# Scratch layout, load shapes and store order around two attention stages of one kernel

## The chip, the cores and the metric

The kernel runs on one core of one Trainium2 chip. Its time is the device time of one execution in microseconds (us). Three runs of the kernel before took 1209.68, 1210.88 and 1212.73 us; the median is 1210.88 us. Engines are named as the profile names them: PE (TensorE matmul), PEld (weight load), DVE (VectorE), ACT (ScalarE), POOL (GpSimd) and SP (SyncE). A small q behind a name (SPq, ACTq) is the engine's sequencer, which issues DMAs.

## The reference

An input x of 2 batches x 1024 tokens x 128 channels passes through four residual layers, all in float32:

```
x = x + attention_a(layernorm(x))      # 16 heads of 8 channels, causal, latent k and v,
                                       # and a 32-channel rotary q.k term shared by all heads
x = x + experts(layernorm(x))          # 8 experts, each takes its top 257 tokens of a batch
x = x + attention_b(layernorm(x))      # 16 heads of 8 channels, causal, plain q, k, v;
                                       # k is reinterpreted by a reshape before q.k
x = x + experts(layernorm(x))
```

In attention_a, `scores = (q.k + q_rope.k_rope) / sqrt(8 + 32)`; q, k and v are products of the normalised x (or of its latent projection) with 128 x 128 weights, reshaped to 16 heads of 8. In attention_b k goes through a transpose and a reshape to (1024, 8), so that a key row of a head is made of other tokens' channels.

## The kernel before

Each attention is one block with two stages, whose kind is "a" or "b". In `project_stage` DVE and ACT normalise x, PE turns it in four chunks of 512 tokens and multiplies it by the weights, ACT copies q and k out of PSUM, rounded to a narrow format, and DVE stores what the rounding left over. So `q_hl` and `k_hl` hold two parts each (0 and 1) as [128 channels, part, 2048 tokens]; for kind "a" the rotary parts `r_hl` lie in the first 64 rows of the third q buffer.

The attention works on 8 groups (2 batches x 4 groups of 4 heads). For each it wants a q tile and a k tile of [128 rows, 4 heads, 1024 tokens] in which the contraction runs down the rows: rows 0 to 95 are three slots of the 32 rotary rows, rows 96 to 119 are three slots of the 8 channels of a head, with parts (0, 0, 1) for q and (0, 1, 0) for k; row 120 holds the row maximum (for q) or ones. The channel rows of a head have to change their partition, and this is done through DRAM: SP stores q_hl, k_hl and r_hl to `scratch_q`, `scratch_k` (kind "b": `scratch_kb`) and `scratch_r` (`store`, L464 to L478), and `load_group` (L293 to L306) brings one group back into one of three buffers: one DMA per slot and side, 12 DMAs for a group of kind "a" whose rotary rows are loaded too, 6 without them. All these DMAs are issued by SP, in its program order: first the stores of group 0 alone, a wait for them, the loads of group 0, then the stores of the three other groups of batch 0, the stores of batch 1, a wait for batch 0, the loads of group 1, and inside `attention_stage` (L538) the maxima of half 1 (`m_rows`), a wait for batch 1 and the loads of group 2.

In `attention_stage` PE first computes the scores of a half (a group and 512 queries) to find their maxima (`max_piece`, L625, reduced on DVE, L762), turns the maxima, DVE copies them, and a DMA (`m_rows`, L535, from ACT for the first half) puts them in row 120. Then it computes the scores again, transposed (`score_unit`, L668), ACT takes the exponential (L739), POOL zeroes the masked triangle, and PE multiplies by v (`values`, L686). A table fixes which max pieces of later halves stand beside which score unit; three score banks let PE run three units ahead of ACT. For kind "a" the rotary rows are loaded for one head, and ACT (group 0, q, L727) or POOL (L581 for group 0, L554 for the next ones) copies them to the other three heads before PE may use the tile. The exponentials are written into the memory of q_hl and k_hl (tiles `pt`), so ACT waits before its first one for all stores of both batches (L728 ff.).

## Time and profile before

| what | value |
|---|---|
| median of three runs | 1210.88 us |
| profiled execution | 1209.04 us, of which the span on the core is 1207.3 us |
| PE busy | 1039.5 us, 86% of the span |
| DVE, ACT, POOL busy | 594.8, 572.0 and 241.9 us |
| DMA | 39.95 MB in 29916 packets, 33 GB/s over the span |
| stage a of attention | about 11 to 411 us of the span |
| stage b of attention | about 631 us on |

The page gives busy times over the whole span; a slice digit of 9 means that PE was busy 90% of it or more. "PEclk" is the granted clock of PE in tenths of 2.4 GHz, so 5 is 1.2 GHz. A timeline row gives the start, the length, the engine, the line, what is written and read, and in brackets how long the engine had been idle and what ended it. A row of a stretch ends with the granted clock, the share of the 16 DMA engines that was busy (0.25 is four of them) and the rate. The profiler's own model of the matmuls makes ends of PE work approximate.

### The profile page before, as it was taken

What the parts mean: (1) busy time and instruction counts of PE and PEld (TensorE: products, weight loads), DVE (VectorE), ACT (ScalarE), POOL (GpSimd) and SP (SyncE); (2) the same over time, 40 slices, a digit from 0 to 9 for tenths busy, and PEclk for the clock granted to TensorE, in tenths of its full rate; (3) what the DMA queues carried; (4) which work ended last, traced back from release to release, by engine and by line L of the source; (5) the groups of instructions that cost most, each with busy time, mean ns of one, the idle gap of its engine ahead of it and who ended that gap; (6) DMA issues with size and microseconds to landing.
All of it is one profiled execution on the core that took longest, in us unless ns stands there. A gap on an engine that the chain in (4) does not pass through costs nothing. (4 is left out here: it accounts for less than half of the span.)

```text
span 1207.3 us, 17627 instructions
## 1 busy us (share of the span) xinstructions
PE 1039.5 (86%) x6814; PEld 754.2 (62%) x6814; DVE 594.8 (49%) x1324; ACT 572.0 (47%) x1031; POOL 241.9 (20%) x488
## 2 busy tenths in 40 slices
PE   2724899999998799999985499999999859999998
PEld 0312555555654688899983255555555348889998
DVE  5624567777770744511124376766776174451111
ACT  1300456666666454444433046666666645444442
POOL 4010342344222100201007011222222210020000
PEclk9965899999999699999997679999999959999999
DMA  3333322321000400000002521211100040000001
GB/s 79 70 93 116 53 28 53 54 46 32 6 1 2 140 1 1 2 1 1 1 1 46 129 44 28 28 27 21 22 14 2 1 140 1 1 2 1 1 1 35
DMA packets 29916, 39.95 MB, mean 33 GB/s; under 512 B 4130, under 2 KB 22218, under 8 KB 29642
## 3 DMA queue, kind: packets, MB, share of 16 engines
q1 hardware_dynamic: 27610, 37.63, 14.7%
q10 hardware_dynamic: 2224, 1.20, 0.5%
q8 instruction: 54, 0.88, 0.3%
q14 instruction: 28, 0.23, 0.1%
HBM read 28.07 MB, written 10.49 MB: 32 GB/s over the span
## 5 line engine op out<-in xcount | busy, mean ns | idle before, releaser
L993 PEld LDWEIGHTS f_banks<-f_w,f_h 128*128 128x128 f32 x2048 | 241.1, 192 | 5.7
L993 PE MATMUL f_banks<-f_w,f_h 128*128 128x128 f32 x2048 | 243.4, 276 | 0.0
L1051 ACT ACTIVATE f_h<-f_banks,b_t 128x512 f32<-128x512 f32 x256 | 172.2, 688 | 144.2 <-PE f_banks L980 140.7
L980 PE MATMUL f_banks<-f_xr,f_w1r 128*128 128x512 f32 x768 | 199.7, 407 | 0.0
L762 DVE TENSOR_REDUCE a_mlate<-a_banks 128x2 f32<-128x1024 f32 (+3 forms) x120 | 124.8, 1079 | 81.3 <-PE a_banks L633 65.4
L980 PEld LDWEIGHTS f_banks<-f_xr,f_w1r 128*128 128x128 f32 x768 | 140.1, 193 | 25.0
L762 DVE TENSOR_REDUCE b_mlate<-b_banks 128x2 f32<-128x1024 f32 (+3 forms) x120 | 124.8, 1079 | 61.7 <-PE b_banks L633 46.4
L625 PE MATMUL a_banks<-a_k,a_q 120*128 120x512 f32 (+3 forms) x384 | 107.1, 384 | 45.2 <-POOL a_q L554 17.3
L1103 DVE SCALAR_TENSOR_TENSOR x<-f_banks,gate,x 128x128 f32<-128x128 f32 x160 | 45.1, 344 | 200.5 <-PE f_banks L993 200.5
L668 PE MATMUL a_banks<-a_q,a_k 121*128 121x512 f32 (+3 forms) x384 | 117.4, 388 | 11.0 <-DMA a_q<-a_mt 9.9
L668 PE MATMUL b_banks<-b_q,b_k 121*128 121x512 f32 (+3 forms) x384 | 116.3, 385 | 11.9 <-DMA b_q<-b_mt 10.2
L625 PE MATMUL b_banks<-b_k,b_q 120*128 120x512 f32 (+3 forms) x384 | 105.8, 380 | 23.9 <-DMA b_q<-scratch_q 11.4
L739 ACT ACTIVATE a_q_hl<-a_banks 128x512 f32<-128x512 f32 (+1 forms) x160 | 81.3, 558 | 59.0 <-PE a_banks L668 57.9
L739 ACT ACTIVATE b_q_hl<-b_banks 128x512 f32<-128x512 f32 (+1 forms) x160 | 81.2, 558 | 53.9 <-PE b_banks L668 52.7
L625 PEld LDWEIGHTS a_banks<-a_k,a_q 120*128 120x128 f32 x384 | 65.8, 206 | 63.6 <-issue 35.5
L739 ACT ACTIVATE a_k_hl<-a_banks 128x512 f32<-128x512 f32 (+1 forms) x160 | 81.3, 559 | 47.7 <-PE a_banks L668 46.6
L739 ACT ACTIVATE b_k_hl<-b_banks 128x512 f32<-128x512 f32 (+1 forms) x160 | 81.3, 559 | 45.8 <-PE b_banks L668 44.3
L668 PEld LDWEIGHTS a_banks<-a_q,a_k 121*128 121x128 f32 x384 | 65.3, 194 | 56.0 <-issue 25.2
L668 PEld LDWEIGHTS b_banks<-b_q,b_k 121*128 121x128 f32 x384 | 64.5, 192 | 56.7 <-issue 23.5
L625 PEld LDWEIGHTS b_banks<-b_k,b_q 120*128 120x128 f32 x384 | 64.9, 203 | 41.9 <-DVE b_mlate L762 18.4
L906 POOL CAST f_w1r<-f_w 128x512 fp32r<-128x512 f32 x16 | 22.8, 1428 | 326.1 <-PE f_banks L980 311.9
L762 DVE TENSOR_REDUCE b_mearly<-b_banks 128x2 f32<-128x768 f32 (+3 forms) x56 | 49.0, 916 | 30.9 <-PE b_banks L633 30.9
(202 smaller groups left out, 1068.2 us busy)
## 6 DMA issues: line engine op xcount, KB each, us to landing
f_w<-in_w SPq DMA_DIRECT2D x32, 256.0 KB, 5.6
a_k<-scratch_k SPq DMA_DIRECT2D x24, 128.0 KB
a_q<-scratch_q SPq DMA_DIRECT2D x24, 128.0 KB
b_k<-scratch_kb SPq DMA_DIRECT2D x24, 128.0 KB
b_q<-scratch_q SPq DMA_DIRECT2D x24, 128.0 KB
a_k<-scratch_r SPq DMA_DIRECT2D x18, 128.0 KB
a_q<-scratch_r SPq DMA_DIRECT2D x18, 128.0 KB
scratch_kb<-b_k_hl SPq DMA_DIRECT2D x16, 128.0 KB, 2.8
```

The lines of the kernel that those rows point to most:

```text
L625: last = pe.matmul(to[:, bank, col:col + w], q2[n % NBUF][0:M0, h, q * P:(q + 1) * P], k2[n % NBUF][0:M0, h, k0:k0 + w], start=True, stop= ...
L668: last = pe.matmul(st[u % NST][:, col:col + w], k2[n % NBUF][0:M0 + 1, h, key * P:(key + 1) * P], q2[n % NBUF][0:M0 + 1, h, c * CH + q0:c ...
L739: act.activation(pt[at % NPT][:, h, 0:cols], st[u % NST][:, 0:cols], ACT.Exp, scale=scale).then_inc(exp_done, 1)
L762: last = dve.tensor_reduce(dst, src, AX.X, ALU.max, negate=True)
L906: pool.tensor_copy(w1r[e % 2][0][:, :], w1[:, e, :]).then_inc(w_high, 1)
L980: last = pe.matmul(h_ps[:, j, :], w1r[e % 2][wp][:, j * P:(j + 1) * P], xr[xp][:, chunk(c)], start=(i == 0), stop=(i == 2))
L993: last = pe.matmul(y_ps[:, q % 2, i * P:(i + 1) * P], h[q % 2][:, j, i * P:(i + 1) * P], w2[:, e, j, :], start=(j == 0), stop=(j == HB - 1))
L1051: act.activation(h[q % 2][:, j, :], h_ps[:, j, :], ACT.Gelu, bias=m.b1_t[:, e * HB + j:e * HB + j + 1]).then_inc(gelu_done, 1)
L1103: last = dve.scalar_tensor_tensor(out=m.x[:, t, :], in0=source(i), scalar=m.gate[:, t * NE + e:t * NE + e + 1], in1=m.x[:, t, :], op0=ALU. ...
```

## The change

Five things change.

1. The scratch in DRAM is laid out as the tiles want it: for each group three slots of 8 channel rows, each row with the 4 heads x 1024 tokens one behind the other (16 KB); `scratch_r` also holds three slots. `load_group` then needs one DMA for the rotary rows of a side (96 rows) and one for its channel rows (24 rows of 16 KB); the k side of kind "b" takes two (16 and 8 rows), since its slots 0 and 2 are the same part. A group costs 4 DMAs (with rotary rows), 2, or 3 (kind "b") in place of 12, 6 and 6.
2. The stores write each slot, so part 0 is stored twice for q and for k of kind "a", and they are made per group, 32 rows at a time.
3. The channels of q and k must come out of the projection in the order group, channel, head. DVE permutes the columns of the weights into `wq` and `wk` at the start of the stage (one or two copies of 128 x 128), and PE waits for these copies before its first q product.
4. In SP's order q of batch 1 comes ahead of its k; kind "b" also puts k of batch 0 behind q of batch 1.
5. The stores of q and of k have semaphores of their own. ACT waits for the q stores before its first exponential, and for the k stores before the third set of exponentials, the first to be written into k_hl.

Some semaphores of the expert layer are merged too (`shifted`, `score_ready` and `gate_ready` become `scored`; `t_turned` and `g_turned` become `rows_turned`); the same instructions wait at the same places.

```diff
@@ -292,17 +292,18 @@
 
 def load_group(eng, m, kind, n, loaded):
 
-    for side, t, slots in (("k", m.k2, KSLOT), ("q", m.q2, QSLOT)):
+    rows = lambda w: w.rearrange("s d (h t) -> (s d) h t", h=GH)
+    for side, t in (("k", m.k2[n % NBUF]), ("q", m.q2[n % NBUF])):
         if rope_load(kind, n):
-            for i, part in enumerate(slots):
-                eng.dma_start(t[n % NBUF][DR * i:DR * (i + 1), 0, :].bitcast(F32),
-                              m.scratch["r"][n // NG, part, "qk".index(side) * DR:("qk".index(side) + 1) * DR, :]).then_inc(loaded[n % NBUF], 16)
-        for i, part in enumerate(slots):
-            if side == "k" and kind == "b":
-                src = m.scratch["kb"][n, part, :, :, :].rearrange("b (h d) s -> b h (d s)", h=GH)
-            else:
-                src = m.scratch[side][n, part, :, :].rearrange("(h d) t -> d h t", d=HD)
-            eng.dma_start(t[n % NBUF][R2 + HD * i:R2 + HD * (i + 1), :, :].bitcast(F32), src
+            eng.dma_start(t[0:R2, 0, :].bitcast(F32),
+                          m.scratch["r"][n // NG, "qk".index(side), :, :, :].rearrange("s d t -> (s d) t")
+                          ).then_inc(loaded[n % NBUF], 16)
+        if side == "k" and kind == "b":
+            both = m.scratch["kb"][n, :, :, :]
+            eng.dma_start(t[R2:R2 + 2 * HD, :, :].bitcast(F32), rows(both)).then_inc(loaded[n % NBUF], 16)
+            eng.dma_start(t[R2 + 2 * HD:M0, :, :].bitcast(F32), rows(both[0:1, :, :])).then_inc(loaded[n % NBUF], 16)
+        else:
+            eng.dma_start(t[R2:M0, :, :].bitcast(F32), rows(m.scratch[side][n, :, :, :])
                           ).then_inc(loaded[n % NBUF], 16)
 
 
...
@@ -323,21 +324,29 @@
...
+    wq = sb("wq", [P, D], F32)
+        wk = sb("wk", [P, D], F32)
...
+    as_rows = lambda w: w.rearrange("p (g d h) -> p g d h", g=NG, h=GH)
+    by_row = lambda w: w.rearrange("p (g h d) -> p g d h", g=NG, h=GH)
...
@@ -351,8 +360,11 @@
         return k_ps if latent else k_ps.rearrange("p (s b) -> p b s", b=HD)
 
     def vector(dve):
+        link = chainer(dve, chain)
+        link(dve.tensor_copy(as_rows(wq[:, :]), by_row(m.w_q[:, :] if latent else m.w_qkv[:, 0:D])))
+        if latent:
+            link(dve.tensor_copy(as_rows(wk[:, :]), by_row(m.w_k[:, :])))
         norm_dve(nc, dve, m, s, st, mv, sc)
-        link = chainer(dve, chain)
         for c in range(NCH):
             tok = slice(c * CH, (c + 1) * CH)
...
                 pe.wait_ge(split, per * (c - 1) + 1)
-            pe.matmul(q_ps, m.w_qkv[:, 0:D] if not latent else m.w_q[:, :], xt,
+            if c == 0:
+                pe.wait_ge(chain, 2 if latent else 1)
+            pe.matmul(q_ps, wq[:, :], xt,
                       start=True, stop=True).then_inc(mm, 1)
             if c + 1 < NCH:
...
-            pe.matmul(k_ps, m.w_k[:, :] if latent else m.w_qkv[:, D:2 * D],
+            pe.matmul(k_ps, wk[:, :] if latent else m.w_qkv[:, D:2 * D],
...
@@ -461,38 +475,58 @@
 
     def sync(sp):
 
-        def store(b, first_group, groups, done):
-            tok = slice(b * T, (b + 1) * T)
-            rows = slice(first_group * GH * HD, (first_group + groups) * GH * HD)
-            to = slice(b * NG + first_group, b * NG + first_group + groups)
-            for i in range(2):
-                sp.dma_start(m.scratch["q"][to, i, :, :], q_hl[rows, i, tok].bitcast(F32)).then_inc(done, 16)
+        def store_q(b, groups, done):
+            for g in groups:
+                for s, part in enumerate(QSLOT):
+                    sp.dma_start(m.scratch["q"][b * NG + g, s, :, :].rearrange("d (h t) -> (d h) t", h=GH),
+                                 q_hl[g * GH * HD:(g + 1) * GH * HD, part, b * T:(b + 1) * T].bitcast(F32)
+                                 ).then_inc(done, 16)
+
+        def store_k(b, groups, done):
+            for g in groups:
+                rows = k_hl[g * GH * HD:(g + 1) * GH * HD, :, b * T:(b + 1) * T].bitcast(F32)
                 if latent:
-                    sp.dma_start(m.scratch["k"][to, i, :, :], k_hl[rows, i, tok].bitcast(F32)).then_inc(done, 16)
+                    for s, part in enumerate(KSLOT):
+                        sp.dma_start(m.scratch["k"][b * NG + g, s, :, :].rearrange("d (h t) -> (d h) t", h=GH),
+                                     rows[:, part, :]).then_inc(done, 16)
                 else:
-                    for g in range(first_group, first_group + groups):
-                        part = k_hl[g * GH * HD:(g + 1) * GH * HD, i, tok].rearrange("p (b s) -> p b s", b=HD)
-                        sp.dma_start(m.scratch["kb"][b * NG + g, i, :, :, :].rearrange("b p s -> p b s"),
-                                     part.bitcast(F32)).then_inc(done, 16)
-                if latent and first_group == 0:
-                    sp.dma_start(m.scratch["r"][b, i, :, :], r_hl[:, i, tok].bitcast(F32)).then_inc(done, 16)
+                    for part in range(2):
+                        sp.dma_start(m.scratch["kb"][b * NG + g, part, :, :].rearrange("b (p s) -> p b s", p=GH * HD),
+                                     rows[:, part, :].rearrange("p (b s) -> p b s", b=HD)).then_inc(done, 16)
+
+        def store_r(b, done):
+            if latent:
+                for s in range(len(QSLOT)):
+                    for i, part in enumerate((QSLOT[s], KSLOT[s])):
+                        sp.dma_start(m.scratch["r"][b, i, s, :, :],
+                                     r_hl[DR * i:DR * (i + 1), part, b * T:(b + 1) * T].bitcast(F32)).then_inc(done, 16)
 
         sp.wait_ge(split, per * 2)
-        store(0, 0, 1, stored_first)
-        sp.wait_ge(stored_first, 16 * (6 if latent else 4))
+        store_r(0, stored_first)
+        store_q(0, [0], stored_first)
+        store_k(0, [0], stored_first)
+        sp.wait_ge(stored_first, 16 * stores_first)
         sp.wait_ge(ones_set, NBUF if latent else 2)
         load_group(sp, m, kind, 0, loaded)
-        store(0, 1, NG - 1, stored[0])
+        store_q(0, range(1, NG), stored_q[0])
+        if latent:
+            store_k(0, range(1, NG), stored_k[0])
         sp.wait_ge(split, per * NCH)
-        store(1, 0, NG, stored[1])
-        sp.wait_ge(stored[0], 16 * stores[0])
+        store_q(1, range(NG), stored_q[1])
+        if not latent:
+            store_k(0, range(1, NG), stored_k[0])
+        store_r(1, stored_k[1])
+        store_k(1, range(NG), stored_k[1])
+        sp.wait_ge(stored_q[0], 16 * stores_q[0])
+        sp.wait_ge(stored_k[0], 16 * stores_k[0])
         if not latent:
             sp.wait_ge(ones_set, 2 * NBUF)
         load_group(sp, m, kind, 1, loaded)
...
             if i == 0:
-                sp.wait_ge(before.stored[1], 16 * before.stores[1])
+                if latent:
+                    sp.wait_ge(before.stored_k[1], 16 * before.stores_k[1])
                 load_group(sp, m, kind, 2, loaded)
+                sp.wait_ge(before.stored_q[1], 16 * before.stores_q[1])
+                sp.wait_ge(before.stored_k[1], 16 * before.stores_k[1])
...
         for b in range(B):
-            act.wait_ge(before.stored[b], 16 * before.stores[b])
+            act.wait_ge(before.stored_q[b], 16 * before.stores_q[b])
...
+                if h == 0 and at == NPT // 2:
+                    for b in range(B):
+                        act.wait_ge(before.stored_k[b], 16 * before.stores_k[b])
...
@@ -1237,9 +1277,10 @@
         m.gate = sb("gate", [P, NT * NE])
         m.vg = [sb(f"vg_{i}", [P, T // P, GH, VW]) for i in range(2)]
         m.weights_in = ctx.enter_context(nc.semaphore("weights_in"))
-        m.scratch = {n: nc.dram_tensor(f"scratch_{n}", (GROUPS, 2, GH * HD, T), F32).ap() for n in "qk"}
-        m.scratch["kb"] = nc.dram_tensor("scratch_kb", (GROUPS, 2, HD, GH * HD, T // HD), F32).ap()
-        m.scratch["r"] = nc.dram_tensor("scratch_r", (B, 2, 2 * DR, T), F32).ap()
+        m.scratch = {n: nc.dram_tensor(f"scratch_{n}", (GROUPS, len(QSLOT), HD, GH * T), F32).ap()
+                     for n in "qk"}
+        m.scratch["kb"] = nc.dram_tensor("scratch_kb", (GROUPS, 2, HD, GH * T), F32).ap()
+        m.scratch["r"] = nc.dram_tensor("scratch_r", (B, 2, len(QSLOT), DR, T), F32).ap()
         constants(nc, ctx, m, a)
         ones_set = ctx.enter_context(nc.semaphore("ones_set"))
         with nc.Block() as block:
```

On SP, the start of stage a before: the stores of group 0, its loads, the first stores behind them. `a_q_hl` and `a_k_hl` are q and k in two parts, `a_q_2` is the q buffer that holds the rotary rows, `a_k_0` and `a_q_0` are the tiles of group 0; a shape is that of the DMA's pattern, the outermost dimension first.

```order
L469 DMA scratch_q<-a_q_hl 32x1024 [waits pa_split]
L471 DMA scratch_k<-a_k_hl 32x1024
L478 DMA scratch_r<-a_q_2 64x1024
L469 DMA scratch_q<-a_q_hl 32x1024
L471 DMA scratch_k<-a_k_hl 32x1024
L478 DMA scratch_r<-a_q_2 64x1024
L298 DMA a_k_0<-scratch_r 32x1024 [waits pa_ones_set,pa_stored_first]
L298 DMA a_k_0<-scratch_r 32x1024 x2
L305 DMA a_k_0<-scratch_k 8x4x1024 x3
L298 DMA a_q_0<-scratch_r 32x1024 x3
L305 DMA a_q_0<-scratch_q 8x4x1024 x3
L469 DMA scratch_q<-a_q_hl 3x32x1024
```

The same place now:

```order
L501 DMA scratch_r<-a_q_2 32x1024 [waits pa_split]
L501 DMA scratch_r<-a_q_2 32x1024 x5
L481 DMA scratch_q<-a_q_hl 32x1024 x3
L490 DMA scratch_k<-a_k_hl 32x1024 x3
L298 DMA a_k_0<-scratch_r 96x1024 [waits pa_ones_set,pa_stored_first]
L306 DMA a_k_0<-scratch_k 24x4096
L298 DMA a_q_0<-scratch_r 96x1024
L306 DMA a_q_0<-scratch_q 24x4096
L481 DMA scratch_q<-a_q_hl 32x1024 x9
L490 DMA scratch_k<-a_k_hl 32x1024 x9
```

Six stores become twelve, all of 32 rows; twelve loads become four, of 96 and 24 rows; the stores behind them are single groups of 32 rows, where three groups had been one DMA with an outermost dimension of 3.

On SP, from the stores of batch 1 to the loads of group 1, stage a, before (`pa_stored0` counts all stores of batch 0 before, `pa_stored_q0` and `pa_stored_k0` below those of q and of k):

```order
L469 DMA scratch_q<-a_q_hl 4x32x1024 [waits pa_split]
L471 DMA scratch_k<-a_k_hl 4x32x1024
L478 DMA scratch_r<-a_q_2 64x1024
L469 DMA scratch_q<-a_q_hl 4x32x1024
L471 DMA scratch_k<-a_k_hl 4x32x1024
L478 DMA scratch_r<-a_q_2 64x1024
L298 DMA a_k_1<-scratch_r 32x1024 [waits pa_stored0]
L298 DMA a_k_1<-scratch_r 32x1024 x2
L305 DMA a_k_1<-scratch_k 8x4x1024 x3
L298 DMA a_q_1<-scratch_r 32x1024 x3
L305 DMA a_q_1<-scratch_q 8x4x1024 x3
```

The same place now:

```order
L481 DMA scratch_q<-a_q_hl 32x1024 [waits pa_split]
L481 DMA scratch_q<-a_q_hl 32x1024 x11
L501 DMA scratch_r<-a_q_2 32x1024 x6
L490 DMA scratch_k<-a_k_hl 32x1024 x12
L298 DMA a_k_1<-scratch_r 96x1024 [waits pa_stored_k0,pa_stored_q0]
L306 DMA a_k_1<-scratch_k 24x4096
L298 DMA a_q_1<-scratch_r 96x1024
L306 DMA a_q_1<-scratch_q 24x4096
```

The six DMAs of batch 1, with an outermost dimension of 4 or 64 rows, become 30 of 32 rows, q first; the loads of group 1 still stand behind them all.

On SP, the start of stage b, before (`scratch_kb` is the reshaped k):

```order
L469 DMA scratch_q<-b_q_hl 32x1024 [waits pb_split]
L475 DMA scratch_kb<-b_k_hl 32x8x128
L469 DMA scratch_q<-b_q_hl 32x1024
L475 DMA scratch_kb<-b_k_hl 32x8x128
L305 DMA b_k_0<-scratch_kb 8x4096 [waits pb_ones_set,pb_stored_first]
L305 DMA b_k_0<-scratch_kb 8x4096 x2
L305 DMA b_q_0<-scratch_q 8x4x1024 x3
L469 DMA scratch_q<-b_q_hl 3x32x1024
L475 DMA scratch_kb<-b_k_hl 32x8x128 x3
L469 DMA scratch_q<-b_q_hl 3x32x1024
```

The same place now:

```order
L481 DMA scratch_q<-b_q_hl 32x1024 [waits pb_split]
L481 DMA scratch_q<-b_q_hl 32x1024 x2
L494 DMA scratch_kb<-b_k_hl 32x8x128 x2
L303 DMA b_k_0<-scratch_kb 16x4096 [waits pb_ones_set,pb_stored_first]
L304 DMA b_k_0<-scratch_kb 8x4096
L306 DMA b_q_0<-scratch_q 24x4096
L481 DMA scratch_q<-b_q_hl 32x1024 x9
L481 DMA scratch_q<-b_q_hl 32x1024 [waits pb_split]
L481 DMA scratch_q<-b_q_hl 32x1024 x11
L494 DMA scratch_kb<-b_k_hl 32x8x128 x14
```

Four stores become five and six loads three; all 21 further stores of q now stand ahead of the 14 of k, with those of batch 1 behind the same wait as before.

## Rows read from the trace of the kernel before

**Rows 1.** The page: PE and its clock in 40 slices of 30.2 us, in tenths.
```profile
PE   2724899999998799999985499999999859999998
...
PEclk9965899999999699999997679999999959999999
```

**Rows 2.** Timeline of PE, stage a: start, us, instruction, idle before, releaser.
```profile
72.44 1.30 PE L625 MATMUL a_banks<-a_k,a_q 120*128 120x384 f32 x4 [15.89 <-POOL a_k L581]
...
92.04 0.79 PE L668 MATMUL a_banks<-a_q,a_k 121*128 121x512 f32 x1 [9.37 <-DMA a_q<-a_mt]
...
107.73 1.05 PE L668 MATMUL a_banks<-a_q,a_k 121*128 121x512 f32 x2
125.43 1.19 PE L625 MATMUL a_banks<-a_k,a_q 120*128 120x512 f32 x2 [16.65 <-POOL a_q L554]
```

**Rows 3.** Timeline of POOL, stage a, the same columns.
```profile
69.29 3.00 POOL L581 CAST a_k<-a_k 96x1024 fp32r<-96x1024 f32 x3 [44.39 <-DMA a_q<-scratch_q]
...
119.36 1.04 POOL L554 CAST a_k<-a_k 96x1024 fp32r<-96x1024 f32 x1 [46.72 <-DMA a_q<-scratch_q]
```

**Rows 4.** Timeline of SP, stage a: its issues of DMAs.
```profile
44.40 0.32 SPq L469 DMA_DIRECT2D scratch_q<-a_q_hl  x1
...
50.79 1.24 SPq L298 DMA_DIRECT2D a_k<-scratch_r  x3
...
59.56 10.78 SPq L471 DMA_DIRECT2D scratch_k<-a_k_hl  x1
...
95.85 6.21 SPq L298 DMA_DIRECT2D a_k<-scratch_r  x3
```

**Rows 5.** Stretches: length, busy PE, PEld, DVE, ACT, POOL; PE clock, DMA share, GB/s.
```profile
45.00:50.00 5.00, 4.51 (x23) 1.98 (x21) 2.85 (x5) 1.71 (x4) 0.00 (x0) 1.00 0.92 200
52.00:53.70 1.70, 1.70 (x6) 0.44 (x6) 0.36 (x1) 1.08 (x3) 0.00 (x0) 1.00 0.77 202
69.00:74.00 5.00, 1.56 (x7) 1.43 (x8) 0.00 (x0) 2.76 (x1) 3.35 (x4) 0.50 0.19 79
79.50:84.00 4.50, 1.92 (x8) 0.78 (x6) 4.07 (x6) 0.00 (x0) 0.00 (x0) 1.00 0.25 103
160.00:169.00 9.00, 8.03 (x58) 4.40 (x58) 5.45 (x7) 4.72 (x9) 0.57 (x2) 1.00 0.52 64
393.00:404.00 11.00, 5.76 (x44) 5.05 (x43) 9.51 (x43) 4.36 (x9) 3.76 (x4) 0.81 1.04 327
650.30:652.50 2.20, 2.20 (x13) 1.43 (x12) 0.69 (x1) 0.94 (x2) 2.14 (x2) 1.00 0.82 179
713.50:717.00 3.50, 3.50 (x36) 2.06 (x35) 2.36 (x2) 2.05 (x5) 0.00 (x0) 1.00 0.58 75
```

**Rows 6.** Timeline of DVE, start of stage a.
```profile
11.78 3.19 DVE L256 BATCH_NORM_STATS2 a_st<-x 128x6 f32<-128x128 f32 x16 [0.32 <-PEq L1245]
...
16.07 2.77 DVE L263 TENSOR_SCALAR a_sc<-a_mv 128x16 f32<-128x16 f32 x1
...
19.62 0.17 DVE L268 TENSOR_TENSOR a_sc<-a_sc 128x16 f32<-128x16 f32 x1
19.83 2.58 DVE L269 TENSOR_SCALAR a_sc<-a_sc 128x16 f32<-128x16 f32 x1
...
22.65 4.99 DVE L272 TENSOR_SCALAR xn<-x,a_mv,a_sc 128x128 f32<-128x128 f32 x16
```

**Rows 7.** Timeline of POOL, the same start.
```profile
11.74 10.64 POOL L450 MEMSET a_k<- 32x4096 f32 x3 [9.20 <-POOLq L1245]
```

**Rows 8.** Timeline of SP, stage b.
```profile
649.02 0.34 SPq L469 DMA_DIRECT2D scratch_q<-b_q_hl  x1
...
653.73 0.95 SPq L305 DMA_DIRECT2D b_k<-scratch_kb  x3
```

**Rows 9.** Timeline of PE, stage b.
```profile
668.48 1.30 PE L625 MATMUL b_banks<-b_k,b_q 120*128 120x384 f32 x4 [11.41 <-DMA b_q<-scratch_q]
...
705.06 1.05 PE L625 MATMUL b_banks<-b_k,b_q 120*128 120x512 f32 x2
```

More of the change, by code:

```diff
@@ L157, in loads_of @@
     buffer_groups = range(n % NBUF, n + 1, NBUF)
-    return sum(6 + (6 if rope_load(kind, g) else 0) for g in buffer_groups)
+    return sum(4 if rope_load(kind, g) else 2 if kind == "a" else 3 for g in buffer_groups)
 def rope_load(kind, n):
@@ L325, in project_stage @@
     chain, first, ones_set, tab_in = sem("chain"), sem("first"), sem("ones_set"), sem("tab_in")
-    stored, stored_first = [sem(f"stored{b}") for b in range(B)], sem("stored_first")
+    stored_q, stored_k = ([sem(f"stored_{side}{b}") for b in range(B)] for side in "qk")
+    stored_first = sem("stored_first")
     latent = kind == "a"
@@ L494, in project_stage @@
     stage.vector, stage.scalar, stage.tensor, stage.gpsimd, stage.sync = vector, scalar, tensor, gpsimd, sync
-    stage.stored, stage.stores, stage.copied, stage.split, stage.splits = stored, stores, copied, split, per * NCH
+    stage.stored_q, stage.stores_q, stage.stored_k, stage.stores_k = stored_q, stores_q, stored_k, stores_k
+    stage.copied, stage.split, stage.splits = copied, split, per * NCH
     return stage
@@ L1130, in vector @@
         link(dve.tensor_reduce(peak[:, :], l, AX.X, ALU.max))
[L1131 removed]
+        dve.tensor_tensor(e_x[:, :, :], l, each(peak[:, :]), ALU.subtract).then_inc(scored, 1)
         dve.wait_ge(exp_done, 1)
```

30 lines of the change are left out of this document (16 added, 14 removed).

## The prediction, written before the changed kernel ran

> **What bounds the kernel now.** I read the page's slices first [rows 1]. PE is busy nine tenths or more nearly everywhere; the low slices are the second to fourth and the 22nd to 24th, the starts of the two attention stages. The change touches only those starts and the DMAs, so the question is what ends PE's waits there. The timeline of PE gives them [rows 2, 9]: in stage a 15.9 us until 72.44 (POOL has copied the rotary rows), 9.4 us until 92.04 (the row maxima arrive) and 16.7 us from 108.78 to 125.43 (POOL again); in stage b 11.4 us until 668.48 (a load). POOL's timeline [rows 3] says that POOL itself had waited for loads: its copies for group 0 start at 69.29, those for group 1 at 119.36. After 125.43 PE is busy nine tenths and waits for no load, so faster loads are worth nothing there. SP's timeline [rows 4, 8] has the reason why loads come late. Stores start at 44.40, the loads of group 0 at 50.79, those of group 1 only at 95.85, behind all stores; one store keeps SP for 10.78 us, as the queue is full.
>
> The rates of the stretches tell which DMAs are slow [rows 5]. Stores of 32 or 64 rows (45 to 50): 200 GB/s with 0.92 of the 16 DMA engines busy. Stores whose pattern begins with 3 (69 to 74): share 0.19, which is three engines, 79 GB/s. Those that begin with 4 (79.5 to 84): 0.25, four engines, 103 GB/s. Loads of 8 channel rows (160 to 169, group 3): 0.52, eight engines, 64 GB/s. Loads of 32 rotary rows (52 to 53.7): 202 GB/s. The expert weights, 128 rows (393 to 404), reach 327 GB/s, so DRAM isn't the limit of the others.
>
> The Trainium skill has the rule behind the shares (DMA: Bandwidth & Descriptors, "Why a DMA increments its semaphore by 16 and not by 1"): a DMA runs on the largest number of engines up to 16 that divides the outermost dimension of both sides. By that rule the three shares come out as seen, and a load of 24 rows would run on 12 engines, a share of 0.75.
>
> **Stores.** One unit is 32 rows of 4 KB, 0.131 MB. Parts stored twice make it half as many bytes again: the first stores of stage a go from 8 units (1.05 MB) to 12 (1.57 MB), the others of stage a from 32 units to 48 (6.29 MB). All are now 32 rows, for which I take 200 GB/s; the ends are 103 (if they were to run like the four-engine ones) and 327. I take 200 because its row holds the same shape, from the same tiles. Issuing them is no limit: SP's first issues take 0.3 to 0.6 us each, about what a unit takes at 200 GB/s (0.66).
>
> **Loads.** Stage a, group 0, before: six rotary units at 202 GB/s are 3.9 us, six channel units at 64 are 12.3, together 16.2 of the 18.4 us from 50.79 to the landing at about 69.2, where ACT and POOL begin; 2.2 us are overhead. Now 0.79 MB of rotary rows take 3.9 us again, and two loads of 24 rows (0.393 MB each) run between 64 GB/s (8 rows) and 202 (32 rows). Eight GB/s a row from the 8-row stretch would be 192; I take 170, 2.3 us each. Sum 3.9 + 4.6 + 2.2 = 10.7 us, 7.7 less. With the two ends it is 18.4 and 10.
>
> **Weight copies.** In stage b POOL does nothing beside them and they cost about 0.3 us (a small DVE instruction takes 0.17 [rows 6]). In stage a POOL clears the three k tiles from 11.74 on, 3.55 us each [rows 7], and two DVE instructions with one source took 2.77 and 2.58 us, ending at 18.84 and 22.41, just where the second and third clearing end (11.74 + 7.1 = 18.84, + 10.64 = 22.38); their neighbour with two sources took 0.17 [rows 6]. A copy is not shown beside a clearing. Bounds: if it doesn't wait, 0.6 us, which the wait of L263 until 18.84 absorbs, so nothing. If each of the two waits for one clearing, they end at about 19.0; statistics follow (4.3 us, 16.07 - 11.78), then the chain to the first xn, which took 3.8 us from 18.84 to 22.65 with a wait of 2.4 in it, so 1.4 to 2: first xn at 25.4 in place of 22.65, less 0.8 since the later xn no longer meet POOL (stage a's sixteen take 4.99). I take the second, +2.0 us, because a copy is a one-source instruction like the two that waited; the end is 3.
>
> The skill says it too (SBUF — State Buffer, "Who interferes with whom"): copy and tensor_scalar between SBUF tiles may take the port pair shared with GpSimd, and the later one waits for the whole instruction. The trace agrees for tensor_scalar; no row has a copy there. It speaks against the change; without it the forecast would be 2 us less.
>
> **Stage a, summed.** First stores start at 44.40 + 2.0 = 46.4. They took 6.39 us for 1.05 MB, so 1.15 beyond 200 GB/s; now 7.9 + 1.15: loads start at 55.4 and land at 66.1. ACT's and POOL's copies of the rotary rows stay 3.2 us: PE starts at 69.4, 3.1 earlier. PE's own road to its third unit (maxima on DVE, the row DMA, max pieces) was 36.3 us (72.44 to 108.78), so it would need group 1 at 105.7. The row maxima travel beside stores as before: there four engines were loaded, now all. Group 1: the 6.29 MB of stores start when the loads' data is through, 65.0, and end at 96.5; its loads (8.5 us of data, 1.1 to land) are in at 106.1; POOL's six copies, 6.07 us (119.36 to 125.43), end at 112.2. PE goes on at 112.2 in place of 125.43: **-13.2 us**. Everything behind that moves with it. The earlier wait for q alone is worth nothing by itself: q of batch 1 is stored at about 86, PE's first unit comes at 89, and PE has three units of room before it needs ACT; k is stored at 97, before the third set. Behind SP's loads of group 1 stand the maxima of half 1 (wanted some 5 us after PE goes on) and the loads of group 2, all with room.
>
> **Stage b, summed.** +0.3 for the copy, five first stores in place of four: 4.71 + 0.7 = 5.4 us, loads from 654.7. Before, three k loads at 75 GB/s (713.5 to 717 [rows 5]) are 5.2 us and three of q at 64 are 6.1, 11.3 of the 14.75 us to PE at 668.48. Now 16 rows at 128 (2.05), 8 rows at 64 (2.05), 24 rows at 170 (2.3): 6.4, with the same 3.4 around them 9.8 us. PE starts at 664.5: **-4.0 us**. Next in line is group 1: 21 units of q at 200 GB/s (13.8 us), 14 of k, whose runs are 512 bytes, at 179 (the stretch from 650.3), 10.3 us, then 6.4 + 1.1 for the load, from 663.5 on: 695. PE wants it at 705.06 - 4.0 = 701, so it is covered by 6 us; without cover each us more costs one.
>
> The expert layers' merged semaphores change no wait, so nothing. Sum: -17.2 us on the profiled execution of 1209.04 is 1191.8. That execution is 1.8 us below the median of the runs, so I forecast **1193 us**.
>
> **Rivals.** What moves the sum most is the store rate r (GB/s): PE goes on in stage a at 72.8 + 7860/r.
> - *Better spread.* The copies don't wait (-2.0), and stores run at 240 GB/s or more (70.8 + 7860/240 = 103.6), between 200 and the 327 of the weights, so that the loads are in when PE asks at 103.7: -21.7, with stage b's -4 to -5 about 1185. Against it: 0.92 of the engines were already busy at 200. 15 in 100.
> - *Duller spread.* Stores at 170 GB/s, since doubled reads of the same 32 rows, loads and the row maxima share the engines: 119.0, -6.4; stage b -3.5; 1201. For it stands the mixed rate of 179; against it nothing but the first stretch. 23 in 100.
> - *The new bytes win: slower.* One mechanism, the half more bytes ahead of group 1's loads. Gain and loss meet at r = 140 (72.8 + 56.1 = 129, which is 3.5 late, what stage b gives). At 103 GB/s, the four-engine rate, stage a would lose 25 us (first stores 15 us, the rest 61) and stage b 13, since its k and q then reach group 1 late: about 1249. For: the change adds stores and I have only one stretch of their shape. Against: that stretch. 8 in 100.
> - *It doesn't do what it says.* A 24-row load as slow as the 8-row ones in rate: two loads take 12.3 us as before, so stage a loses 7.7 twice (group 0 and 1) of its 13.2, less what PE's later need covers, and stage b is unchanged or late: 1206. 4 in 100.
>
> **Numbers.** Forecast case 50 in 100, its own spread 1189 to 1197. The range for 8 in 10 takes in the duller and most of the better spread: 1184 to 1204. This kernel's runs tell 0.3% (3.6 us) from no change: faster 0.89, same 0.05, slower 0.06; the last two share the slow rival and the slow tail of the duller one.
>
> **What would show it.** First xn at 25 us and not 22.7; the two copies about 3.5 us each. Stores at a share near 0.9 and 200 GB/s from 66 to 96; loads of 24 rows at a share of 0.75, 2.3 us each. POOL's copies of group 1 start at 106, PE's wait before L625 of group 1 is 6 to 7 us in place of 16.7. In stage b PE starts at 664 to 665 and waits for no load at group 1. I am wrong if the stretch of stores runs below 140 GB/s, if PE waits for the k stores through ACT, or if the spans behind both starts, which I leave as they are, change length.

## The result, and the profile after

| | before | changed kernel |
|---|---|---|
| median of the runs | 1211.18 us (1209.68 to 1212.73, 4 runs) | 1176.82 us (1176.40 to 1181.03, 4 runs) |
| span of the profiled execution | 1207.3 us | 1175.5 us |
| ratio | | 0.9724, 95% interval 0.9699 to 0.9750 |

The sign was right, the size was not: 1193 us (1184 to 1204) was forecast, so the kernel gained 34 us where I had worked out 17. The mean granted clock of the spans is 0.932 before and 0.941 after.

PE's timeline of the changed kernel (start, us, instruction, idle before and releaser; L662 and L705 are what L625 and L668 were) answers to [rows 2, 9]:

```profile
68.09 1.30 PE L662 MATMUL a_banks<-a_k,a_q 120*128 120x384 f32 x4 [11.41 <-POOL a_k L618]
...
84.71 0.79 PE L705 MATMUL a_banks<-a_q,a_k 121*128 121x512 f32 x1 [6.32 <-DMA a_q<-a_mt]
...
103.11 1.19 PE L662 MATMUL a_banks<-a_k,a_q 120*128 120x512 f32 x2 [1.66 <-POOL a_q L591]
...
640.47 1.30 PE L662 MATMUL b_banks<-b_k,b_q 120*128 120x384 f32 x4 [6.40 <-DMA b_q<-scratch_q]
...
655.38 0.80 PE L705 MATMUL b_banks<-b_q,b_k 121*128 121x512 f32 x1 [5.18 <-DMA b_q<-b_mt]
...
671.93 1.05 PE L662 MATMUL b_banks<-b_k,b_q 120*128 120x512 f32 x2
```

Subtract the rows of before. In stage a PE starts 4.4 us earlier (3.1 forecast) and goes on with group 1 at 103.11 in place of 125.43: 22.3 us, where 13.2 were forecast. In stage b it starts 28.0 earlier, but its first L705 is 33.1 earlier: the trip of the row maxima, from PE's start to its first score unit, takes 14.9 us there in place of 20.0. The forecast left that trip as it was.

SP's and POOL's timelines answer to [rows 3, 4, 8]:

```profile
44.52 2.64 SPq L501 DMA_DIRECT2D scratch_r<-a_q  x6
...
54.75 0.30 SPq L298 DMA_DIRECT2D a_k<-scratch_r  x1
...
56.36 4.62 SPq L481 DMA_DIRECT2D scratch_q<-a_q_hl  x9
...
85.99 0.31 SPq L298 DMA_DIRECT2D a_k<-scratch_r  x1
...
626.02 1.26 SPq L481 DMA_DIRECT2D scratch_q<-b_q_hl  x3
```
```profile
64.94 3.00 POOL L618 CAST a_k<-a_k 96x1024 fp32r<-96x1024 f32 x3 [40.28 <-DMA a_q<-scratch_q]
...
97.04 1.04 POOL L591 CAST a_k<-a_k 96x1024 fp32r<-96x1024 f32 x1 [28.75 <-DMA a_q<-scratch_q]
```

The loads of group 1 are issued at 85.99 where the sum had 96.5, and POOL starts on them at 97.04 in place of 106.1. The later stores are issued from 56.36 on, while the loads of group 0 are on their way (until 64.9). The stretches show what the engines did then:

```profile
45.00:50.00 5.00, 4.63 (x23) 1.97 (x21) 2.75 (x4) 1.71 (x4) 0.00 (x0) 1.00 0.91 197
...
56.00:64.00 8.00, 0.67 (x7) 0.48 (x5) 2.78 (x5) 0.60 (x1) 0.00 (x0) 0.81 0.97 247
64.00:86.00 22.00, 10.08 (x36) 6.89 (x37) 8.51 (x10) 3.15 (x2) 3.35 (x4) 0.58 0.94 257
```

The first row confirms the rate that I carried over, 197 GB/s. The other two don't: 247 GB/s while loads and stores share the engines, and 257 GB/s for the stores behind them. The 257 is no steady rate, as its first four microseconds show:

```profile
64.00:68.00 4.00, 0.00 (x0) 0.00 (x0) 0.00 (x0) 2.76 (x1) 3.06 (x4) 0.50 0.94 363
```

From 68 to 86 the stores ran at 234 GB/s.

SP's load issues in the middle of stage a tell about the stretch that I had left alone. Before:

```profile
192.09 1.25 SPq L298 DMA_DIRECT2D a_k<-scratch_r  x3
...
294.04 0.96 SPq L305 DMA_DIRECT2D a_k<-scratch_k  x3
```

After:

```profile
169.48 0.32 SPq L298 DMA_DIRECT2D a_k<-scratch_r  x1
...
268.62 0.29 SPq L306 DMA_DIRECT2D a_k<-scratch_k  x1
```

The three groups between these marks took 101.95 us and now take 99.14, so the lead grows from 22.6 to 25.4 us. At stage b's first store it is 23.0 (649.02 - 626.02). The whole account is: 22.3 us at group 1 of stage a, 3.1 in its later groups (2.8 of them between these marks), 2.4 lost again before stage b, then 5.0 to PE's start and 5.1 by the maxima there, 1.3 lost behind. That makes the 31.8 us between the two spans.

### The profile page after: what moved, and what is told of

It is laid out like the page before. It is cut to its first block and busy times, and to the rows that moved or that the text cites. A ratio compares the mean times of both kernels' runs of the same rounds, so it can differ in the third digit from the quotient of the medians.

```text
span 1175.5 us, 17618 instructions
## 1 busy us (share of the span) xinstructions
PE 1040.7 (89%) x6814; PEld 756.3 (64%) x6814; DVE 593.8 (51%) x1327; ACT 572.1 (49%) x1031; POOL 243.1 (21%) x488
## 5 line engine op out<-in xcount | busy, mean ns | idle before, releaser
L662 PE MATMUL a_banks<-a_k,a_q 120*128 120x512 f32 (+3 forms) x384 | 107.7, 386 | 25.4 <-POOL a_k L618 11.4
L705 PE MATMUL a_banks<-a_q,a_k 121*128 121x512 f32 (+3 forms) x384 | 117.1, 388 | 7.7 <-DMA a_q<-a_mt 6.6
L662 PE MATMUL b_banks<-b_k,b_q 120*128 120x512 f32 (+3 forms) x384 | 106.3, 381 | 18.7 <-DVE b_mlate L802 7.9
L705 PE MATMUL b_banks<-b_q,b_k 121*128 121x512 f32 (+3 forms) x384 | 116.6, 386 | 6.9 <-DMA b_q<-b_mt 5.2
L705 PEld LDWEIGHTS a_banks<-a_q,a_k 121*128 121x128 f32 x384 | 65.3, 194 | 52.6 <-issue 23.5
L705 PEld LDWEIGHTS b_banks<-b_q,b_k 121*128 121x128 f32 x384 | 64.9, 193 | 51.8 <-issue 23.5
L662 PEld LDWEIGHTS a_banks<-a_k,a_q 120*128 120x128 f32 x384 | 66.1, 207 | 43.8 <-DVE a_mlate L802 17.8
L662 PEld LDWEIGHTS b_banks<-b_k,b_q 120*128 120x128 f32 x384 | 65.1, 203 | 36.5 <-DVE b_mlate L802 18.2
L802 DVE TENSOR_REDUCE a_mearly<-a_banks 128x2 f32<-128x768 f32 (+3 forms) x56 | 49.0, 914 | 28.3 <-PE a_banks L670 28.3
```

Of the source, the lines that this page charges most:

```text
L662: last = pe.matmul(to[:, bank, col:col + w], q2[n % NBUF][0:M0, h, q * P:(q + 1) * P], k2[n % NBUF][0:M0, h, k0:k0 + w], start=True, stop= ...
L705: last = pe.matmul(st[u % NST][:, col:col + w], k2[n % NBUF][0:M0 + 1, h, key * P:(key + 1) * P], q2[n % NBUF][0:M0 + 1, h, c * CH + q0:c ...
L802: last = dve.tensor_reduce(dst, src, AX.X, ALU.max, negate=True)
```

## The experiments

Each kernel was timed beside the kernel before, whose median was 1211.0 to 1211.8 us in the three sets. The trips are the times from PE's start on group 0 to its first score unit, differences of two PE rows such as those above. The last column is the time at which PE goes on with group 1 in stage a; "no wait" means that POOL was ready before PE asked.

| kernel | median us | ratio, 95% interval | trip a | trip b | PE goes on, stage a |
|---|---|---|---|---|---|
| before | 1211.2 | 1 | 19.6 | 20.0 | 125.4 |
| split_stores | 1201.4 | 0.9928 (0.9905 to 0.9950) | 23.5 | 24.3 | 109 |
| maxima_first | 1192.5 | 0.9851 (0.9819 to 0.9884) | 15.1 | 15.0 | 110.7 |
| grouped_stores | 1226.9 | 1.0141 (1.0116 to 1.0165) | 18.4 | 21.7 | 140.0 |
| changed kernel | 1176.8 | 0.9724 (0.9699 to 0.9750) | 16.6 | 14.9 | 103.1 |
| loads_alone | 1181.3 | 0.9749 (0.9730 to 0.9769) | 16.6 | 15.7 | 109.3 |
| copies_on_act | 1175.5 | 0.9719 (0.9692 to 0.9747) | 16.2 | 16.0 | 102.3 |
| all_awaited | 1178.3 | 0.9734 (0.9710 to 0.9759) | 15.9 | 16.6 | 105.4 |
| early_one | 1177.7 | 0.9726 (0.9694 to 0.9759) | 19.7 | 18.3 | no wait |
| rope_once | 1173.8 | 0.9706 (0.9672 to 0.9741) | 15.8 | 21.9 | 99.5 |
| half_stores | 1173.0 | 0.9693 (0.9663 to 0.9722) | 16.0 | 15.7 | 100.1 |
| two_issuers | 1174.1 | 0.9693 (0.9672 to 0.9713) | 16.0 | 14.4 | 102.3 |
| three_edits | 1169.2 | 0.9648 (0.9628 to 0.9667) | 16.5 | 15.8 | no wait |
| four_edits | 1168.2 | 0.9644 (0.9624 to 0.9664) | 15.7 | 14.4 | no wait |

**split_stores** (from before: only the stores are split)

```diff
-        store(0, 1, NG - 1, stored[0])
+        for g in range(1, NG):
+            store(0, g, 1, stored[0])
...
-        store(1, 0, NG, stored[1])
+        for g in range(NG):
+            store(1, g, 1, stored[1])
```

> The kernel before with one edit: the stores of the later groups go out one group (32 rows) at a time, each part once, old layout, old loads of 8 rows. Theory 1 (the spread over the engines is what the stores gain, and the row maxima fly faster because of it): the 32 later units of stage a run beside and behind the loads of group 0 at about 249 GB/s, so group 1's loads are issued at 76 to 78 in place of 95.85, land near 98, and PE goes on at about 104 to 106 in place of 125.4; in stage b the trip from PE's start to its first L668 falls from 20.0 to 15 us. Together 20 to 26 us less than before, about 1187 us. Theory 2 (the new layout carries the gain, few large loads above all): under 10 us of gain, and the trip in stage b stays at 20.

The kernel takes 9.6 us less, where theory 1 had 20 to 26 and theory 2 under 10. The first half of theory 1 came true: group 1's loads are issued at 77.21, POOL starts on them at 94.04, and PE reaches its third unit at 109.10 without a wait. Its second half was false, and so was theory 2's unchanged trip: both trips grew by 4 us. PE's timeline and two stretches of it:

```profile
93.84 0.80 PE L670 MATMUL a_banks<-a_q,a_k 121*128 121x512 f32 x1 [12.74 <-DMA a_q<-a_mt]
...
681.24 0.79 PE L670 MATMUL b_banks<-b_q,b_k 121*128 121x512 f32 x1 [13.58 <-DMA b_q<-b_mt]
```
```profile
77.00:82.00 5.00, 3.84 (x10) 1.41 (x8) 4.71 (x6) 0.00 (x0) 0.00 (x0) 0.50 0.87 188
82.00:92.00 10.00, 0.00 (x0) 0.00 (x0) 0.00 (x0) 0.00 (x0) 0.00 (x0) 0.50 0.58 101
```

ACT issues the maxima from 81.96 on, and SP issued group 1's 12 loads from 77.2 to 82.3. While PE waits, the share is 0.58 at 101 GB/s, near the half that 8-row loads occupy [rows 5]. So the next experiment kept those loads away from the maxima.

**maxima_first** (from split_stores)

```diff
# end of the projection stage, SP
-        load_group(sp, m, kind, 1, loaded)
# begin of the attention stage, SP
+        sp.wait_ge(m_in[0], 16 * GH)
+        load_group(sp, m, kind, 1, loaded)
```

> The kernel before with its later stores split by group (as split_stores), and group 1's loads issued only once the row maxima of half 0 have landed. In split_stores those loads (8 rows each, eight engines) were issued just ahead of the row maxima, and the trip from PE's start to its first L670 was 23.5 us in stage a and 24.3 in b. Theory 1 (the maxima wait behind whatever is queued on the few engines they use, here the 8-row loads): both trips fall to 15 or 16 us. In stage a group 1's loads then start 8 to 9 us later and give the time back (PE goes on near 109 as before); in stage b they are in by 687 on the clock of split_stores, when PE asks at about 688, so stage b gains 8 to 9 us: about 1192 us. Theory 2 (the maxima wait for other traffic, the stores on all engines or DRAM): the trips stay above 20 us and the later loads cost 5 us or more: 1205 or worse.

Theory 1 came true to the microsecond: both trips are 15 us and the time is 1192.5.

```profile
86.86 0.79 PE L671 MATMUL a_banks<-a_q,a_k 121*128 121x512 f32 x1 [5.12 <-DMA a_q<-a_mt]
...
110.72 1.19 PE L628 MATMUL a_banks<-a_k,a_q 120*128 120x512 f32 x2 [7.10 <-POOL a_q L557]
...
673.64 0.79 PE L671 MATMUL b_banks<-b_q,b_k 121*128 121x512 f32 x1 [4.47 <-DMA b_q<-b_mt]
```

PE waits about 5 us for the maxima with nothing ahead of them (in stage a the DMA engines moved nothing from 82 to 84). In the changed kernel, whose stores keep the engines nearly full, it waits 5.2 to 6.3 us. In the kernel before it waited 9.4 us in stage a, where the stores ran at a share of 0.25, and 10.2 in stage b, where k's stores of 32 rows ran beside q's of four groups (0.52 to 0.61). So it isn't traffic as such that holds the maxima: 207 GB/s (79 to 82 in the changed kernel) delay them less than 99 GB/s (88 to 92 before). Split stores and this order, in the old layout, give 19 of the 34 us. The other 15 come with the layout and its loads (PE starts at 68.09 and not 71.80 in stage a, and goes on at 103.11 and not 110.72); no run tries the new load shapes by themselves.

**grouped_stores** (from the changed kernel)

```diff
+        def several(side, hl, slots, b, groups, done):
+            to = slice(b * NG + groups[0], b * NG + groups[-1] + 1)
+            rows = slice(groups[0] * GH * HD, (groups[-1] + 1) * GH * HD)
+            for s, part in enumerate(slots):
+                sp.dma_start(m.scratch[side][to, s, :, :].rearrange("g d (h t) -> g (d h) t", h=GH),
+                             hl[rows, part, b * T:(b + 1) * T].bitcast(F32)).then_inc(done, 16)
```

> The changed kernel with one edit: stores of the later groups go out as one DMA per slot over three or four groups, as before. Theory 1 (spread): at 79 and 103 GB/s the later stores of stage a take some 60 us, group 1's loads are issued near 120, PE goes on near 137 in place of 103.1 (+34); in stage b group 1's load comes 8 us late and the trip of the row maxima is back at 20 us in place of 14.9. About 1217 us, slower than before. Theory 2 (layout): at most 10 us more than the changed kernel.

Theory 1 came true and more: PE goes on at 140.00 (137 expected), the trips are 18.4 and 21.7 us (20 expected in stage b), and the time is 1226.9 us where 1217 was expected, 16 us more than before. Its stretches show the three- and four-engine shares of [rows 5] again:

```profile
68.00:82.00 14.00, 7.31 (x31) 4.41 (x30) 8.42 (x10) 0.00 (x0) 0.00 (x0) 0.74 0.22 88
```

With split_stores this makes a square: the split alone is worth -10 us, the layout (with the other parts of the change) alone +16, both together -34. Writing half more bytes pays only where the stores spread over all the engines; this is the rival "the new bytes win", which the split keeps away.

**loads_alone** (from the changed kernel)

```diff
         load_group(sp, m, kind, 0, loaded)
+        sp.wait_ge(loaded[0], 16 * loads_of(kind, 0))
         store_q(0, range(1, NG), stored_q[0])
```

> The changed kernel, with the later stores held until group 0's loads have landed, so that loads and stores no longer share the engines there. Theory 1 (the prediction missed that the stores run beside the loads and fill the engines' gaps; a stream of 32-row stores alone runs at the 200 to 210 GB/s that it used): the loads land 2 to 4 us earlier, then 6.29 MB of stores take 30 us, group 1's loads are issued near 93 and PE goes on near 110 in place of 103.1, as the prediction's own sum had it (112.2). Time 6 to 9 us more than the changed kernel, some of it less by the earlier start of PE: about 1183. Theory 2 (the rate of the stores itself is 250 or more): PE goes on at 104 or before, within 2 us of the changed kernel.

Its SP and its stretches:

```profile
65.26 4.31 SPq L481 DMA_DIRECT2D scratch_q<-a_q_hl  x9
...
92.78 0.31 SPq L298 DMA_DIRECT2D a_k<-scratch_r  x1
```
```profile
55.00:64.00 9.00, 1.90 (x12) 0.97 (x8) 3.48 (x6) 0.60 (x1) 0.00 (x0) 0.85 0.76 175
66.00:92.00 26.00, 16.19 (x48) 9.98 (x49) 13.03 (x15) 3.91 (x3) 2.73 (x4) 0.50 0.91 228
```

This kernel does what my sum assumed, loads first and stores behind them, and PE goes on at 109.29, 6.2 us later than in the changed kernel. The time is 1181.3 us, where 1183 was expected. So theory 1 holds, except that the loads didn't land 2 to 4 us earlier: they take 10.2 us with the engines to themselves and 10.1 us with stores beside them.

It splits the error in two. The first part is 6.8 us at group 1's load issue (92.78 - 85.99), the price of keeping loads and stores apart. About half of it are stores that pass beside the loads: in the changed kernel 2.38 MB had moved from 54.5 to 64.9 (229 GB/s), of which 1.57 are the loads, so 0.81 MB of stores, 3.5 us at 229 GB/s. The other half is the change from one to the other: from 63.5 to 66 loads_alone moved nothing, and from 64.9 to 68 the changed kernel ran at 349 GB/s. What allows that burst was not tried; from 68 to 86 both kernels ran at 234. The second part is the rate: 6.29 MB in 27.5 us are 229 GB/s, where I had carried over 200 (31.5 us), so 4.0 us.

**copies_on_act** (from the changed kernel)

```diff
-        link(dve.tensor_copy(as_rows(wq[:, :]), by_row(...)))
+        act.activation(as_rows(wq[:, :]), by_row(...), ACT.Copy).then_inc(w_set, 1)
...
-                pe.wait_ge(chain, 2 if latent else 1)
+                pe.wait_ge(w_set, 2 if latent else 1)
```

> The changed kernel with the weight copies on ACT in place of DVE. DVE's statistics then start near 11.8 and the first xn stands near 22.7 again. Theory 1 (the copies' 2 us are given back by PE's clock, which rises at the same moment in both kernels): the first store stays within 0.3 us of 44.5 and the time within 1 us of the changed kernel. Theory 2 (the 2 us are a real cost, as in the prediction): first store near 42.5, 2 us less in all.

Theory 1, nearly: the first xn stands at 22.73, 2 us before that of the changed kernel, but the first store comes at 44.94, 0.4 later, and the median is 1.4 us lower, with intervals that overlap almost wholly. DVE and PE of the changed kernel, then PE of this one:

```profile
11.61 3.55 DVE L364 COPY a_wq<-w_q 128x128 f32<-128x128 f32 x1 [0.32 <-PEq L1286]
...
24.72 4.19 DVE L272 TENSOR_SCALAR xn<-x,a_mv,a_sc 128x128 f32<-128x128 f32 x16
...
28.91 1.72 PE L430 MATMUL a_banks<-xt,a_wq 128*128 128x512 f32 x2
...
30.91 1.02 PE L438 MATMUL a_banks<-a_ckv,a_wk 128*128 128x512 f32 x2
```
```profile
27.88 1.92 PE L431 MATMUL a_banks<-xt,a_wq 128*128 128x512 f32 x2
...
30.43 1.91 PE L439 MATMUL a_banks<-a_ckv,a_wk 128*128 128x512 f32 x2
```

The copies do wait for POOL's memsets, 3.55 us each as forecast. But the first chunk's matmuls run at half their later speed (1.91 us a pair, then 1.02), though the granted clock of the stretch reads 1.00. Here they start at 23.60 and are slow until about 32; in the changed kernel they start at 25.12 and are slow only until about 30.5. The earlier start is used up by more work at the slow speed. Why the speed changes there is left open.

**all_awaited** (from the changed kernel)

```diff
+        for g in range(1, NG):
+            store_q(0, [g], stored_q[0])
+            store_k(0, [g], stored_k[0])
         sp.wait_ge(split, per * NCH)
+        store_r(1, stored_k[1])
+        for g in range(NG):
+            store_q(1, [g], stored_q[1])
+            store_k(1, [g], stored_k[1])
...
             act.wait_ge(before.stored_q[b], 16 * before.stores_q[b])
+            act.wait_ge(before.stored_k[b], 16 * before.stores_k[b])
```

> The changed kernel with q and k of a group stored in turn, and ACT waiting for all of them before its first exp. Theory 1 (the prediction: storing q first and waiting for it alone is worth nothing): within 1.5 us of the changed kernel. Theory 2: the first exp comes 2 to 4 us later in each stage and the end moves with it, 3 us or more.

ACT's first exp comes 4.6 us later in stage a (from 85.61 to 90.19), PE goes on 2.3 us later, and the time is 1.5 us more, at the edge of theory 1 and inside the uncertainty. Storing q first isn't where the gain is.

**early_one** (from the changed kernel)

```diff
+        store_k(0, range(1, NG), stored_k[0])
+        sp.wait_ge(stored_q[0], 16 * stores_q[0])
+        sp.wait_ge(stored_k[0], 16 * stores_k[0])
+        load_group(sp, m, kind, 1, loaded)
         sp.wait_ge(split, per * NCH)
         store_q(1, range(NG), stored_q[1])
```

> The changed kernel with group 1's load issued as soon as batch 0 is stored, ahead of batch 1's stores. Theory 1 (only the 1.7 us for which PE still waits for POOL in stage a are to be had, and the row maxima travel beside stores as before): PE goes on at 100 to 101 in place of 103.1, stage b unchanged, about 1175 us. Theory 2 (the maxima now meet the load on 12 engines, as they met the 8-row loads in split_stores): the trip from PE's start to the first L705 grows by 3 us or more in one or both stages, and the time is that of the changed kernel or worse.

Theory 2 came true: PE no longer waits for POOL, but the trips grow by 3.0 and 3.4 us, and the time is that of the changed kernel.

```profile
87.80 0.80 PE L702 MATMUL a_banks<-a_q,a_k 121*128 121x512 f32 x1 [9.74 <-DMA a_q<-a_mt]
...
658.21 0.80 PE L702 MATMUL b_banks<-b_q,b_k 121*128 121x512 f32 x1 [7.53 <-DMA b_q<-b_mt]
```

**rope_once** (from the changed kernel)

```diff
-                for s in range(len(QSLOT)):
-                    for i, part in enumerate((QSLOT[s], KSLOT[s])):
+                for part in range(2):
+                    for i in range(2):
...
+            eng.dma_start(t[pair:pair + 2 * DR, 0, :].bitcast(F32), both.rearrange("s d t -> (s d) t")
+                          ).then_inc(loaded[n % NBUF], 16)
+            eng.dma_start(t[one:one + DR, 0, :].bitcast(F32), both[0, :, :]).then_inc(loaded[n % NBUF], 16)
```

> The changed kernel with the rotary rows stored once in place of by slot, and loaded by two DMAs of 64 and 32 rows in place of one of 96. Theory 1 (bytes decide: two units of 0.131 MB less ahead of group 0's loads, two more less ahead of group 1's): PE starts 1.2 us earlier and goes on in stage a 1.5 to 2.5 us earlier; stage b as it is. About 1175 us. Theory 2 (the overlap of issue and transfer hides the duplicates, or the further DMAs cost it back): no difference in where PE starts, within 0.5 us.

PE starts 1.5 us earlier and goes on 3.6 us earlier, more than theory 1 had, though the interval of the ratio overlaps that of the changed kernel. The profiled execution took 1177.86 us, 4 us more than the median, since in it stage b, which the edit doesn't touch, lost 7 us: SP issued group 1's load at 648.81, between ACT's four issues of the maxima (647.14 to 650.09), and PE waited 11.12 us. In the changed kernel the load was issued at 654.10, 0.4 us behind the last of them. Nothing in the program orders the two, so a small shift decides it.

**half_stores** (from the changed kernel)

```diff
+        for c in range(2):
+            sp.wait_ge(split, per * (c + 1))
+            at = (c * CH, (c + 1) * CH)
+            store_q(0, [0], stored_first, *at)
+            if latent:
+                store_k(0, [0], stored_first, *at)
+                store_r(0, stored_first, *at)
```

> The changed kernel, with group 0's first stores cut in two by tokens, so that the first half goes out after the first chunk (near 37 us) beside the second chunk's matmuls. In stage b only q is cut. Theory 1 (stage a's start is one chain of bytes behind the second chunk's end: half of 1.57 MB leaves it): group 0's loads are issued near 50 in place of 54.75, PE starts near 63.3 in place of 68.1, group 1's loads start near 81 and PE goes on near 98 in place of 103.1; stage b gains about 1. Sum 5 to 6 us less than the changed kernel, about 1171 us. Theory 2 (runs of 2 KB in place of 4 KB and twice as many issues on SP use it up): under 2 us.

The result lies between the theories: group 0's loads are issued at 52.28 (50 expected), PE goes on at 100.10 (98 expected), and the time is 3.8 us less by the medians, though the intervals overlap. SP's issues of twelve more DMAs may take a part of it.

**two_issuers** (from the changed kernel)

```diff
-        m_rows(act, 0)
+        m_rows(act, 0, range(0, GH, 2))
...
         copy_v(0)
+        m_rows(pool, 0, range(1, GH, 2), m_pool)
```

> The changed kernel with the four DMAs of half 0's row maxima issued by two engines, two by ACT and two by POOL, which waits there for group 1's load anyway. Theory 1 (ACT's four issues, 3.2 us in stage a and 2.6 in b, stand on the path, and half of them goes): the trip from PE's start to the first L705 is 1.3 to 1.6 us shorter; in stage a PE then waits longer for POOL's copies and nothing is gained, in stage b 1.3 us: about 1175.5. Theory 2 (the maxima wait on the DMA engines behind the stores, whoever issues them, or POOL's issue is slower): trips as they are or longer, no gain.

The trips are 0.6 and 0.5 us shorter, less than theory 1 had. The median is 2.8 us lower, which those trips don't explain; the intervals overlap, so it may be chance. This is left open.

**three_edits**, **four_edits** (the diffs of half_stores, rope_once and maxima_first on the changed kernel, and in the second that of two_issuers too; where they meet:)

```diff
+        sp.wait_ge(m_in[0], 32)
+        sp.wait_ge(m_pool, 32)
+        load_group(sp, m, kind, 1, loaded)
```

> The changed kernel with three edits at once: group 0's first stores cut in two by tokens (half_stores, 3.8 us less than the changed kernel by the medians), the rotary rows stored once (rope_once, 3.0 less), and group 1's loads issued only once the row maxima of half 0 are in (maxima_first). If they add up: PE starts near 64.5 in place of 68.1, both trips are 15 to 16 us (rope_once alone had one of 21.9 in stage b, where group 1's loads went out among the maxima), PE goes on in stage a near 97. About 1168 us. If half_stores and rope_once save the same bytes' time twice, 1171 to 1173.

> three_edits and two_issuers together. Group 1's loads wait for the maxima here, so in both stages what shortens the maxima's trip counts: if two issuers save 1.3 to 1.6 us a trip, 2 to 3 us less than three_edits, about 1166; if they save nothing, the same as three_edits within 1.5 us.

The three edits give 1169.2 us (1168 was expected if they add up), with an interval wholly below that of the changed kernel. PE starts at 65.64 (64.5 expected), both trips are near 16, and no wait for POOL stands at group 1. The fourth edit adds 1 us, not distinguishable from nothing. So there is a version that is faster than both kernels, by 7.7 us against the changed one.

## Why the prediction was wrong in size

- **Where the time would come from**: right. PE's gains at its starts make up nearly all of the difference.
- **Stores**: this step failed: "the 6.29 MB of stores start when the loads' data is through, 65.0, and end at 96.5". The stores start beside the loads, which leave a quarter of the engines idle, and run on without a gap when the loads are in (together 6.8 us, loads_alone), and the stream ran at 229 GB/s and not at the 200 of a stretch in which all stores read rows 0 to 63 of their tiles (4.0 us). By the prediction's own formula, PE at 72.8 + 7860/r, the observed 103.1 is r = 259: a value that belonged to the rival *better spread*, which I had given 15 in 100. Its mechanism isn't what happened, though: the copies did wait, and no steady stream of stores reached its 240 GB/s.
- **Row maxima**: this step failed too. "The row maxima travel beside stores as before: there four engines were loaded, now all." I had seen that they share engines and costed it at nothing. PE's wait for them is 5 us with nothing ahead (maxima_first), 8 to 11 beside stores that take three or four groups in one DMA (the kernel before, grouped_stores), and 13 behind 8-row loads (split_stores). Some of that is ACT's own work: in stage b its four issues take 2.60 us in place of 4.09, and the maxima are in 1.65 us after the last issue in place of 5.19, together 5.0 of the 5.1 us by which the trip shrank. These DMAs of four rows are issued by ACT and not by SP, so what they share with the stores are the DMA engines. The runs fit a wait for what lies ahead on the few engines that such a DMA uses; which engines these are, no view counts. In stage a the shorter trip (16.6 us in place of 19.6) was hidden, as POOL was later.
- **Weight copies**: the 3.55 us each were right, xn came 2.1 us later, and the first store only 0.1 us later. The term of +2.0 was worth nothing, since the matmuls that started later spent less time at half speed. The rule of the Trainium skill (SBUF — State Buffer, "Who interferes with whom"), that a copy can take the port pair shared with GpSimd, and that whichever comes later then waits for the whole instruction, is what this trace shows (3.55 and 3.53 us for copies that take 0.27 in stage b); it decides the duration, not the price.
- **Loads**: right in stage a (10.1 us, 10.7 forecast). In stage b PE starts 14.45 us after the first store, where 15.2 was the sum.
- **The stretches left unchanged**: "waits for no load" was wrong for batch 1's groups. POOL waits for the load ahead of its masks, and PE for the masks. The waits of POOL and PE in one group of the kernel before, and POOL's in the changed one:

```profile
243.14 3.02 POOL L554 CAST a_k<-a_k 96x1024 fp32r<-96x1024 f32 x3 [13.44 <-DMA a_q<-scratch_q]
...
247.30 1.07 PE L686 MATMUL a_banks<-a_k_hl,vg 128*32 128x512 f32 x8 [0.95 <-POOL a_k_hl L575]
```
```profile
213.37 3.02 POOL L591 CAST a_k<-a_k 96x1024 fp32r<-96x1024 f32 x3 [6.56 <-DMA a_q<-scratch_q]
```

  Two such waits (0.95 and 0.83 us), which the changed kernel doesn't have, are 1.8 of the 2.8 us; the rest I can't explain. Nor can I explain the 2.4 us lost between 268.62 and 626.02. PE is busy 1.5 us longer there (330.8 in place of 329.3 us), at a mean granted clock of 0.95 in place of 0.96.
- **Arithmetic of the miss**: 9.1 us in stage a (group 1's loads are issued 10.5 earlier than in the sum, which is 6.8 + 4.0 less the 0.3 by which the stores of loads_alone start behind 65.0; the loads themselves took 11.05 us in place of 9.6 and give 1.4 back), 5.1 by the maxima, about 1 by stage b's loads: together the 15 us between -17.2 and -31.8. That SP begins 1.9 us before the 46.4 of the sum brought little of it, since the first twelve units took 10.2 us and not 9.0.
- **The rivals**: the slow one comes true without the split (grouped_stores). Its price in stage a was put at 25 us where the formula gives 24, which changes nothing. Storing q first is worth no more than 1.5 us (all_awaited), as forecast.

## What to carry to other kernels

Count a queue of DMAs in bytes on the engines and not as a row of steps: a transfer that leaves engines idle hides a part of what is queued behind it, and a wait between two transfers leaves a gap. Before a small DMA is called unchanged, ask what is queued on its own few engines when it is issued, and make the large load wait for it rather than leave the order to chance. Here a DMA with an outer dimension of 3 or 4 delayed not only itself but also the small DMAs beside it.
